# Message passing over a sorted edge list: when GpSimd waits for its scatters in the sort

## The chip, the cores and the metric

One core of one Trainium2 chip runs the whole program. The metric is the device time of one execution in microseconds. The core's engines run side by side: TensorE (PE in the profile, PEld for its weight loads), VectorE (DVE), ScalarE (ACT), GpSimd (POOL) and SyncE (SP, which here only issues DMAs). They meet through semaphores.

## The reference

The input is a graph of 12500 nodes with 128 features and 200000 edges; each edge has a source, a destination, 16 attributes and a type. `src` and `dst` are the edges' ends. The edges arrive sorted by destination.

```python
edge_index = jnp.stack([src, dst])
x = _layernorm(x + _L0(x, edge_index, edge_type_9, ...))   # messages summed per destination, then a GRU cell
x = _layernorm(x + _L1(x, edge_index, edge_attr_16, ...))  # three GIN layers
# _L0: messages = segment_sum(h[src] @ W_msg.T + b_msg + edge_embed[type], dst)
# _L1, per layer: agg = segment_sum(concat(x[dst], edge_attr @ enc_w + enc_b), src), self loops added,
#      then two matrix products with a batch norm and a relu between them
```

Everything that touches edges is a gather of node rows and a sum over the edges of a node. The kernel turns a large part of it into dense products with counts: how many edges lead from a node of one block to a node of another.

## The kernel before, in words

The 200000 edges lie in 1563 tiles of 128 edges, one edge per partition. The program has three stages: the **sort** (which also builds the counts), the first layer with its GRU cell, and three GIN layers. All engines go through the stages in the same order, each with its own program.

**The sort.** The tiles are taken in 25 windows (class `Window`), of 56 tiles in window 0, 64 in windows 1 to 23 and 35 in window 24. For each group of four tiles VectorE makes one-hot rows of the source block (`rank_onehot`, L1976), TensorE counts them up over the partitions (`ranks_tensor`, L2703 to L2709), VectorE copies the carry (L2052), multiplies (L2053, which raises the semaphore `prod` once per group) and reduces (L2065) to the rank of each edge within its source block. At the end of a window `window_places` computes each edge's slot in a table in DRAM and writes it as an integer (L1968), which raises `placed`. Windows 0 and 1 are cut into three and two pieces that are placed one by one.

**The scatters.** GpSimd takes the pieces in order. For each tile it issues one indirect DMA (L3017) that scatters 128 records of 20 words of four bytes, 80 bytes each, from the buffer `RECA` to their slots in the table `RAd` (rec_q in the profile). There are 1563 of them. Before a piece GpSimd waits for `placed` and for the records (`rec_made`, written by ScalarE, three buffers that go round by window). Inside a window the tiles go in fours ("quads"), and two more waits stand there. One paces the scatters of a window beside the ranking of the window after it: at the first tile of a quad GpSimd waits until VectorE has finished a certain group of that window (`ranked_beside`, on `prod`). The other one holds GpSimd to its landings: all scatters of a quad raise one of two semaphores of the buffer, even quads the first and odd quads the second, by 16 each when they have landed (`scat[q % 3][quad % 2]`), and at the second tile of every quad but the first GpSimd waits for all four scatters of the quad before.

**Who waits for the scatters.** ScalarE refills a record buffer only when the scatters of the window three before have landed (`records_scalar`, L2432; it is issued at the seventh group of the window before). SyncE reads the sorted records back for the counts (`cell_records_sync`, L3071 and L3076), two ranges of destinations at a time, when the windows that hold them have landed. The units of this work (375, `cells_vector`, `cells_tensor`, `cells_scalar`, `cells_sync`) start in window 4 and are spread beside the ranking at 18 units a window: VectorE makes one-hot rows (L2028, L2034), TensorE multiplies them into counts (L2733) and multiplies the counts with node features (L2750), ScalarE copies the counts out (L2457, L2461), and SyncE transposes them by DMA (L3115, 360 of them) and stores them (L3124). The next stage starts when all scatters have landed: VectorE, SyncE and GpSimd each wait for that at its head (L2219, L3225, L3024).

**After the sort.** GpSimd gathers node rows for the edges that the counts leave out (L3033 in the first layer, L3051 in the GIN layers); TensorE multiplies counts with node features (L2965). These lines aren't touched by the change.

Of the kernel before, what the change touches and what calls it, by code (L numbers as in the profile page):

```python
# [27 lines left out]
GT = 4  # L28
# [121 lines left out]
def ranked_beside(x, tile):  # L150

    w = x.w if x.b < x.w.n else WIN[x.w.q + 1]
    return x.w.g0 + x.b // GT + (tile - x.first) // GT * w.groups // 16 - 1
# [157 lines left out]
def scattered(q, part):  # L311

    return 16 * sum(1 for i in range(q % 3, q + 1, 3) for k in range(tiles_in(i)) if k // GT % 2 == part)


def scattered_to(q, quad):

    return (scattered(q - 3, quad % 2) if q >= 3 else 0) + 16 * GT * (quad // 2 + 1)
# [61 lines left out]
def summed_beside(r):  # L380

    return max(2 * r - 2, GATHERED[QS0 + r - QR] + 1 if r >= QR else 0)
# [7 lines left out]
def stored(g):  # L390

    return 16 * (g // 2 + 1)


def tiles_of(q, tiles):
    return min(GT, tiles - GT * q)
# [72 lines left out]
def gathered_stored(lay, i):  # L469

    return 16 * max(k // 2 + 1 for k in range(SG * (lay - 1), SG * (lay - 1) + SG - J) if k % 2 == i)
# [1087 lines left out]
def program(nc, x, dst, src, typ, ea, wmsgT, wihT, whhT, emb, bmsg, bih, bhh, encT, w1a, w1b, w2, pv, out):  # L1559
    ctx = ExitStack()  # L1560
    with ctx:
# [5 lines left out]
        def sem(name):  # L1567
            made_sems.append(Sem(ctx.enter_context(nc.semaphore(name))))
            return made_sems[-1]
# [191 lines left out]
        scat = [[sem(f"scattered{i}_{part}") for part in range(2)] for i in range(3)]  # L1761
# [1234 lines left out]
        def quick_gpsimd(g):  # L2996
            g.iota(IOTA[:], [[1, P]], base=0, channel_multiplier=0, allow_small_or_imprecise_dtypes=True).then_inc(*iotas.inc())
            g.iota(DIF[:], [[1, P]], base=0, channel_multiplier=-1, allow_small_or_imprecise_dtypes=True).then_inc(*iotas.inc())
            g.iota(I258[:, :, 0:86], [[86, 3], [1, 86]], base=0, channel_multiplier=0, allow_small_or_imprecise_dtypes=True).then_inc(*iotas.inc())
            g.iota(POSF, [[1, CP]], base=TRASH, channel_multiplier=NTQ, allow_small_or_imprecise_dtypes=True).then_inc(*iotas.inc())  # L3000
            g.iota(N0B, [[P, 100], [0, 16]], base=-P, channel_multiplier=0, allow_small_or_imprecise_dtypes=True).then_inc(*iotas.inc())
            g.iota(IO256[:], [[1, 256]], base=0, channel_multiplier=0, allow_small_or_imprecise_dtypes=True).then_inc(*iotas.inc())
            g.iota(I132[:, :, 0:44], [[44, 3], [1, 44]], base=0, channel_multiplier=0, allow_small_or_imprecise_dtypes=True).then_inc(*iotas.inc())
            g.wait_ge(nulls.sem, 16 * NULLS_FIRST)
            for x in PIECES:
                q, a = x.w.q, WIN[x.w.q - 1].end if x.w.q else 0
                if q == NULLS_FIRST // 2 and x.first == a:
                    g.wait_ge(nulls_rest.sem, 16 * (TRASH // 49 - NULLS_FIRST))
                g.wait_ge(placed.sem, x.n + 1)
                g.wait_ge(rec_made.sem, 3 + 3 * (q + 1))  # L3010
                for c in range(x.first, x.end):
                    quad = (c - a) // GT
                    if q < 24 and (c - x.first) % GT == 0 and ranked_beside(x, c) > x.w.g0 + x.b // GT:
                        g.wait_ge(prod.sem, ranked_beside(x, c))
                    if quad and (c - a) % GT == 1:
                        g.wait_ge(scat[q % 3][(quad - 1) % 2].sem, scattered_to(q, quad - 1))
                    g.indirect_dma_start(  # L3017
                        out=RAd, out_offset=bass.IndirectOffsetOnAxis(ap=POSI[:, c:c + 1], axis=0),
                        in_=RECA[q % 3][:, c - a, :], in_offset=None).then_inc(*scat[q % 3][quad % 2].inc(16))
            for i in range(4):  # L3020
                g.wait_ge(m_out[i].sem, 16 * len(range(i, SG * J, 4)))
            for i in range(3):
                for part in range(2):
                    g.wait_ge(scat[i][part].sem, scattered(24 - (24 - i) % 3, part))  # L3024
            g.wait_ge(weights_dve.sem, 4)
            for i in range(2):
                g.wait_ge(xp_out[i].sem, stored(SG - 1 - i) + 16 * (i == 0))
            for q in range(QS0, NQ0):
                r = q - QS0
                if summed_beside(r) > 0:  # L3030
                    g.wait_ge(q0_sum.sem, summed_beside(r))
                for i in range(tiles_of(q, C)):
                    g.indirect_dma_start(  # L3033
                        out=XG[:, r % QR, i, 0:3 * P], out_offset=None, in_=XPd,
                        in_offset=bass.IndirectOffsetOnAxis(ap=SRCi[:, GT * q + i:GT * q + i + 1], axis=0)).then_inc(*rows_in[r % QR].inc(16))
            g.wait_ge(idx_made.sem, 2 * (NS // IX))
            for i in range(2):
                g.wait_ge(x1_out[i].sem, stored(SG - 1 - i))
                g.wait_ge(pc_out[i].sem, stored(SG - 1 - i))
                g.wait_ge(xt_out[i].sem, stored(SG - 1 - i))  # L3040
            for lay in range(3):
                if lay:
                    for i in range(2):
                        g.wait_ge(hb_out[i].sem, gathered_stored(lay, i))
                for x in GRP[SG * lay:SG * (lay + 1)]:
                    for r in range(x.group0, x.group0 + x.groups):
                        a = K * (4 * x.u + (r - x.group0) // 2) + TO[r % 2]
                        if r >= LR:
                            g.wait_ge(row_sum.sem, r - LR + 1)
                        for i in range(TS[r % 2]):  # L3050
                            g.indirect_dma_start(  # L3051
                                out=GL[:, r % LR, i, 0:3 * P], out_offset=None, in_=HGd[lay],
                                in_offset=bass.IndirectOffsetOnAxis(ap=IDXA[:, a + i:a + i + 1], axis=0)).then_inc(*rows_in[r % LR].inc(16))
            g.wait_ge(row_sum.sem, 3 * QL)
            g.sem_inc(*done.inc())
# [318 lines left out]
        quick_scalar(nc.scalar)  # L3374
        quick_tensor(nc.tensor)
        quick_gpsimd(nc.gpsimd)
        quick_sync(nc.sync)

# [81 lines left out]
```

## Time and profile before

| | |
|---|---|
| time, median of 3 runs | 6228.43 us (6224.02 to 6235.12) |
| span of the profiled execution | 6981.5 us (no other time of this execution is listed) |
| the sort, in the profiled execution | from 0 to 2676.5 us |
| POOL busy, whole span | 4213.9 us (60%), 4243 instructions |
| DVE busy, whole span | 3769.9 us (54%) |
| PE busy, whole span | 5386.3 us (77%) |

A row of the profile names a line, an engine and an operation, the tiles that it writes and reads, and how long the engine was idle ahead of it, with what ended that idle time. "issue" means that the engine waited for nothing that the profile shows. "remote", and on the chain "another core or an unknown queue", means that a semaphore came up at that moment and that no recorded instruction explains when. The profiled execution is 753.1 us longer than the median of the runs.

### The profile page before, as it was taken

The page shows a single profiled execution, that of the slowest core. Times are in us where ns is not written, and L with a number is a line of the kernel's source. Part 1 is how long each engine was busy: PE and PEld are TensorE (multiplying, and loading weights), DVE is VectorE, ACT ScalarE, POOL GpSimd, SP SyncE. Part 2 cuts the span into 40 slices and gives each one's busy share as a digit, 9 for nine tenths or more (in the row PEclk, how much of TensorE's full clock was granted, in tenths as well). Part 3 has the DMA queues.
Part 4 walks back from the last instruction along what each step waited for, and adds up shares of the span by engine and source line. Part 5 has one row for each costly group of instructions (what it writes and reads, how often), then busy time and mean ns, then how long its engine had stood idle before and what let it go on. Part 6 is the DMA issues. An engine that isn't in the chain of part 4 may idle for free.

```text
span 6981.5 us, 88118 instructions
## 1 busy us (share of the span) xinstructions
PE 5386.3 (77%) x26429; PEld 3361.9 (48%) x26429; DVE 3769.9 (54%) x14165; ACT 3302.5 (47%) x4432; POOL 4213.9 (60%) x4243
## 2 busy tenths in 40 slices
PE   4376767676766764666676999999898998898998
PEld 1133333333333322333344666666666666666666
DVE  8576767777766754455566444443333333444443
ACT  1164545555655641122122666665555554554554
POOL 5655555555555556666631666666676666666665
PEclk5588988888988985677776999999999999999999
DMA  7165556556655652333323666667666667666665
GB/s 250 48 144 129 140 121 138 127 134 136 157 127 127 148 138 76 98 101 102 100 78 121 188 190 185 194 196 220 184 186 179 190 191 217 184 184 174 177 185 148
DMA packets 1068177, 1066.40 MB, mean 153 GB/s; under 512 B 494051, under 2 KB 784501, under 8 KB 1067701
## 3 DMA queue, kind: packets, MB, share of 16 engines
q1 hardware_dynamic: 889573, 782.05, 40.1%
q0 software_dynamic: 178128, 278.65, 16.0%
q8 instruction: 220, 3.60, 0.2%
q14 instruction: 256, 2.10, 0.1%
HBM read 747.21 MB, written 216.68 MB: 138 GB/s over the span
## 4 chain that ended last, share of the span: by engine, by line
PE 44%; another core or an unknown queue 6%; DVE 4%; issue 4%; ACT 2%; DMA 1%; SPq 0%; DVEq 0%; ACTq 0%
PE ps L2965 27%; PE ps L2935 4%; PE ps L2848 2%; PE ps L2899 2%; PE ps L2809 2%; PE ps L2810 1%; DVE BIG L2197 1%; PE ps L2909 1%; PE ps L2910 1%; PE ps L2811 1%; ACT MSR L2575 1%; DVE MSR L2258 0%; PE ps L2812 0%; PE ps L2914 0%
## 5 line engine op out<-in xcount | busy, mean ns | idle before, releaser
L3051 POOL DMA_INDIRECT GL<-h_gathered,IDXA x2058 | 2112.6, 1027 | 1227.7 <-issue 568.5
L2965 PE MATMUL ps<-MSR,HP 128*128 128x512 f32 (+1 forms) x9000 | 2375.0, 410 | 174.9 <-ACT MSR L2575 71.2
L3017 POOL DMA_INDIRECT rec_q<-BIG x1563 | 1513.7, 968 | 1156.2 <-issue 473.6
L2575 ACT CAST MSR<-MS 128x1024 fp32r<-128x1024 uint8 (+1 forms) x1500 | 1491.8, 1028 | 1272.9 <-PE ps L2965 820.3
L2965 PEld LDWEIGHTS ps<-MSR,HP 128*128 128x128 f32 x9000 | 1675.6, 195 | 624.9 <-issue 168.5
L2750 PE MATMUL ps<-MTB,XPS 128*128 128x512 bf16 x4410 | 1312.2, 416 | 1.1 <-DMA XPS<-x_parts 0.8
L2258 DVE CAST MSR<-MS 128x1024 fp32r<-128x1024 uint8 (+1 forms) x750 | 522.6, 699 | 1236.7 <-PE ps L2965 738.5
L2457 ACT CAST MT<-ps 128x512 uint16<-128x512 f32 x735 | 427.4, 582 | 959.2 <-remote 633.3
L2461 ACT CAST MTB<-MT 128x1024 bf16<-128x1024 uint8 x735 | 767.9, 1045 | 64.8 <-PE ps L2750 10.3
L3033 POOL DMA_INDIRECT BIG<-x_parts,SRCq x611 | 582.8, 954 | 341.5 <-issue 164.4
L2750 PEld LDWEIGHTS ps<-MTB,XPS 128*128 128x128 bf16 x4410 | 439.7, 103 | 248.7 <-issue 68.1
L2935 PE MATMUL ps<-GL,SL 128*128 128x384 bf16 (+1 forms) x2058 | 456.0, 338 | 8.9 <-issue 7.3
L2709 PE MATMUL ps<-BIG 128*128 128x392 f16 x435 | 165.2, 380 | 354.4 <-DVE BIG L2052 269.1
L2733 PE MATMUL ps<-BIG 128*128 128x256 bf16 x738 | 215.5, 293 | 286.8 <-DVE BIG L2034 83.7
L2034 DVE TENSOR_SCALAR BIG<-I,BIG 128x258 bf16<-128x258 f16 x982 | 335.0, 399 | 188.3 <-remote 162.5
L2197 DVE TENSOR_SCALAR BIG<-IO,DREL 128x256 bf16<-128x256 f16 x1579 | 352.7, 299 | 94.2 <-remote 84.6
L2239 DVE TENSOR_SCALAR SL<-IOTH,RELA 128x128 bf16<-128x128 f16 x2058 | 387.1, 263 | 0.0
L1976 DVE TENSOR_SCALAR BIG<-IOTM,BIG 128x98 f16<-128x98 f16 x1804 | 346.5, 254 | 0.0
L2809 PE MATMUL ps<-WE,BIG 10*128 10x512 f32 x196 | 166.3, 940 | 197.7 <-ACT XMT L2522 158.8
L2052 DVE CAST BIG<-ps 128x98 f16<-128x98 f32 x435 | 109.6, 252 | 306.9 <-remote 288.0
L2733 PEld LDWEIGHTS ps<-BIG 128*128 128x128 bf16 x738 | 77.6, 105 | 395.7 <-issue 179.7
L2935 PEld LDWEIGHTS ps<-GL,SL 128*128 128x128 bf16 x2058 | 154.7, 98 | 229.3 <-issue 166.2
(248 smaller groups left out, 6244.4 us busy)
## 6 DMA issues: line engine op xcount, KB each, us to landing
MS<-counts SPq DMA_DIRECT2D x1080, 256.0 KB
counts<-BIG SPq DMA_DIRECT2D x360, 256.0 KB
XPS<-x_parts SPq DMA_DIRECT2D x192, 384.0 KB
GL<-h_gathered,IDXA POOLq DMA_INDIRECT x2058
rec_q<-BIG POOLq DMA_INDIRECT x1563
rec_q<-BIG SPq DMA_DIRECT2D x44, 490.0 KB, 10.4
HTI<-h_cols SPq DMA_DIRECT2D x72, 256.0 KB
h_dense<-PCL SPq DMA_DIRECT2D x30, 512.0 KB
```

The lines of the kernel that those rows point to most:

```text
L2197: got = v.tensor_scalar(hot[:, i, :], IO256[:, :], DREL[:, GT * q + i:GT * q + i + 1], None, ALU.is_equal)
L2239: got = v.tensor_scalar(SL[:, r % LR, i, :], IOTH[:, :], RELA[:, q + i:q + i + 1], None, ALU.is_equal)
L2258: v.tensor_copy(MSR[:, g % RM, :, 0:w].rearrange("p t (c s) -> p t c s", s=P), MSB[:, i % MR, 0:4 * w].rearrange("p (c h s t) -> p h t c s ...
L2457: s.copy(MT[:, m % 3, 512 * i:512 * (i + 1)].bitcast(U16), PS[PAIR[(p0 + i) % 2]][:, :]).then_inc(*mt_out.inc())
L2461: s.copy(MTB[:, m % 3, 1024 * i:1024 * (i + 1)], MT[:, m % 3, 512 * i:512 * (i + 1)].bitcast(U8)).then_inc(*mtb.inc())
L2575: s.copy(MSR[:, g % RM, :, 0:w].rearrange("p t (c s) -> p t c s", s=P), MSB[:, i % MR, 0:4 * w].rearrange("p (c h s t) -> p h t c s", h=2, ...
L2750: got = t.matmul(PS[6 + x.j % 2][:, :], XPS[:, x.load % 3, i, part, :], MTB[:, m % 3, 512 * i:512 * (i + 1)], start=4 * x.u + i + part == ...
L2935: got = t.matmul(bank[:, 0:w], SL[:, r % LR, i, :], GL[:, r % LR, i, 0:w], start=at + i == 0, stop=at == 1 and i == TS[1] - 1, skip_group_ ...
L2965: got = t.matmul(bank[:, 0:w], HP[:, d, part, :], MSR[:, g % RM, d % 2, 0:w], start=d + part == 0, stop=lay > 0 and d + part == BD, skip_g ...
L3017: g.indirect_dma_start(out=RAd, out_offset=bass.IndirectOffsetOnAxis(ap=POSI[:, c:c + 1], axis=0), in_=RECA[q % 3][:, c - a, :], in_offset ...
L3033: g.indirect_dma_start(out=XG[:, r % QR, i, 0:3 * P], out_offset=None, in_=XPd, in_offset=bass.IndirectOffsetOnAxis(ap=SRCi[:, GT * q + i: ...
L3051: g.indirect_dma_start(out=GL[:, r % LR, i, 0:3 * P], out_offset=None, in_=HGd[lay], in_offset=bass.IndirectOffsetOnAxis(ap=IDXA[:, a + i: ...
```

## The change

GpSimd's wait for its landings moves from the second tile of a quad to the first, and asks for the quad before the last one instead of the last one. It stands from the third quad of a window on. All else is the same: the number of scatters, their order, the semaphores that they raise, and the other waits.

```diff
                     if q < 24 and (c - x.first) % GT == 0 and ranked_beside(x, c) > x.w.g0 + x.b // GT:
                         g.wait_ge(prod.sem, ranked_beside(x, c))
-                    if quad and (c - a) % GT == 1:
-                        g.wait_ge(scat[q % 3][(quad - 1) % 2].sem, scattered_to(q, quad - 1))
+                    if quad >= 2 and (c - a) % GT == 0:
+                        g.wait_ge(scat[q % 3][quad % 2].sem, scattered_to(q, quad - 2))
                     g.indirect_dma_start(
                         out=RAd, out_offset=bass.IndirectOffsetOnAxis(ap=POSI[:, c:c + 1], axis=0),
                         in_=RECA[q % 3][:, c - a, :], in_offset=None).then_inc(*scat[q % 3][quad % 2].inc(16))
```

Before, at most five scatters of a window were on their way at once (a quad and the first of the next); now at most eight. `scattered_to(q, quad)` gives the semaphore's value when that quad of window q has landed.

## Rows read from the trace of the kernel before

**Rows 1.** The page: the span, and the chain of waits by engine.

```profile
span 6981.5 us, 88118 instructions
...
PE 44%; another core or an unknown queue 6%; DVE 4%; issue 4%; ACT 2%; DMA 1%; SPq 0%; DVEq 0%; ACTq 0%
```

**Rows 2.** Line L3017 over the whole span: count, min/median/max ns, what ended idle time.

```profile
L3017 POOL DMA_INDIRECT rec_q<-BIG x1563: 952/958/1733, 22.7 to 2674.4; - x196
...
  DVE BIG L1968: 209.3, 16
```

**Rows 3.** GpSimd's waits up to 302 us: us in total, times, longest us.

```profile
POOL rec_q L3017 <- issue: 53.5, 162, 1.5
POOL rec_q L3017 <- DMA rec_q<-BIG: 36.5, 13, 4.9
```

**Rows 4.** GpSimd's waits from 302 to 2632 us.

```profile
POOL rec_q L3017 <- issue: 410.1, 1155, 4.6
POOL rec_q L3017 <- DMA rec_q<-BIG: 224.2, 126, 4.7
POOL rec_q L3017 <- DVE BIG L2053: 202.1, 55, 12.8
```

**Rows 5.** GpSimd in order of time at the sort's end: start us, us, [idle before].

```profile
2582.26 0.96 POOL L3017 DMA_INDIRECT rec_q<-BIG  x1 [6.82 <-DVE BIG L2053]
...
2591.46 0.96 POOL L3017 DMA_INDIRECT rec_q<-BIG  x1 [3.14 <-DMA rec_q<-BIG]
...
2632.72 0.96 POOL L3017 DMA_INDIRECT rec_q<-BIG  x1 [0.30 <-issue]
...
2674.38 0.96 POOL L3017 DMA_INDIRECT rec_q<-BIG  x1 [0.30 <-issue]
```

**Rows 6.** The chain of waits in order of time there: start us, us, what.

```profile
2674.38 2.09 DMA rec_q<-BIG
```

**Rows 7.** Busy time of each engine, windows 3 to 23 of the ranking.

```profile
core 0: us, PE busy (x) PEld busy (x) DVE busy (x) ACT busy (x) POOL busy (x), PEclk, DMA share, GB/s
302.80:2526.10 2223.30, 1546.48 (x8845) 793.92 (x8845) 1596.81 (x6143) 1198.70 (x1578) 1239.07 (x1285) 0.85 0.58 135
```

**Rows 8.** VectorE's waits in that stretch: us in total, times, longest us.

```profile
DVE BIG L2052 <- remote: 227.7, 64, 10.8
DVE BIG L2034 <- remote: 162.5, 43, 13.1
DVE WE L2034 <- remote: 102.1, 29, 13.3
DVE PC L1994 <- remote: 29.1, 2, 16.9
```

**Rows 9.** VectorE in order of time at the sort's end.

```profile
2593.01 0.56 DVE L2053 TENSOR_TENSOR BIG<-ps,BIG 128x392 f32<-128x392 f32 x1
...
2620.23 0.18 DVE L1968 CAST BIG<-BIG 128x35 int32<-128x35 f32 x1
...
2676.91 0.09 DVE L2221 MEMSET BIG<- 128x1 f32 x2 [36.37 <-DMA rec_q<-BIG]
```

**Rows 10.** VectorE and GpSimd in order of time where window 2's places are ready.

```profile
196.32 0.20 DVE L1968 CAST BIG<-BIG 128x64 int32<-128x64 f32 x1
...
217.38 0.95 POOL L3017 DMA_INDIRECT rec_q<-BIG  x1 [0.30 <-issue]
```

**Rows 11.** ScalarE's waits in the stretch of rows 7.

```profile
ACT BIG L2440 <- DMA BIG<-rec_q: 95.9, 1, 95.9
ACT MT L2457 <- DMA BIG<-MT: 17.1, 9, 2.9
```

**Rows 12.** DMA queues from 1000 to 1250 us: packets, MB, share of 16 engines.

```profile
q0 software_dynamic: 4672, 1.50, 4.0%
...
rec_q<-BIG POOLq DMA_INDIRECT x148
```

**Rows 13.** The same stretch of the ranking: the transposes of the counts.

```profile
L3115 SPq DMA_TRANSPOSE BIG<-MT x360: 1113/1238/3040, 324.4 to 2522.7; - x180
```

## The prediction

> **What bounds the kernel now.** I read the page first for the span and the chain of waits, then the line of the scatters, then the waits by engine for the sort in pieces, then the order of time at the sort's end.
>
> The chain ends at the last scatter: the record of L3017 at 2674.38 us, 2.09 us until it has landed [rows 6], and behind it VectorE, idle for 36.37 us, starts the next stage [rows 9]. So at its end the sort is bound by GpSimd. Before that the profiled execution shows GpSimd waiting for VectorE, not the other way: 202.1 us on its pace [rows 4] and 209.3 us on the places of a window [rows 2]. VectorE in turn is busy for 1596.8 of the 2223.3 us from window 3 to 23 [rows 7] and idle for 521.4 us on "remote" (227.7 + 162.5 + 102.1 + 29.1) [rows 8]. It is full up with work and with waits that no recorded instruction explains.
>
> What is bound in the timed runs is another question, since the profiled execution's span (it lists no other time) is 753 us longer than their median; the sums below are made in the profiled execution and carried over to the median through this difference. Had the two only the unexplained waits between them, then this is how they divide. The chain from 2674 us on holds 6% of the span as "another core or an unknown queue" [rows 1], 419 us (5.5 to 6.5%: 384 to 454). The other 753 - 419 = 334 us (299 to 369) must then be missing from the sort, which takes 2676.5 - 334 = 2342 us (2307 to 2377) in a timed run.
>
> GpSimd's own chain, with no wait for VectorE in it, comes out nearly as long. The last 34 scatters stand 1.262 us apart ((2674.38 - 2632.72) / 33, rows 5): 0.958 of work and 0.30 between. 1563 of them [rows 2] take 1973 us, from 22.7 us on [rows 2]. Waits for landings: up to 302 us 36.5 us in 13 rows [rows 3], less 0.30 each is 33; after that 224.2 in 126 [rows 4], 186. Some of these waits have no releaser and stand under "issue": 53.5 + 410.1 us over 162 + 1155 rows [rows 3, 4], less 0.30 each, 68 more at most. Landings so cost 219 to 287 us, and the whole is 22.7 + 1973 + 219 to 287 + 2.1 = 2217 to 2285 us. Against 2342 (2307 to 2377) GpSimd has 22 to 160 us to spare in 25 windows: about one to six us in a hundred. I take it to be on the path for part of the sort.
>
> **The change, part by part.** It adds and removes no instruction but the wait. Nothing passes another queue: the wait and the scatters stay on GpSimd, in the same order, and what is queued behind the wait is the quad itself, and behind that the next window's, for which ScalarE's refill, SyncE's read-back and the next stage wait.
>
> *The landings.* The old wait costs nothing if the last scatter of a quad lands within two steps, 2.53 us from its start; when it stands, the landing takes those 2.53 us and the wait, less the 0.30 of every step, on top. The mean wait is 224.2 / 126 = 1.8 us, the longest 4.9 [rows 3, 4], so the landings take 4.0 us in the mean and at most 7.1. The new wait asks for that scatter five steps after its start, 6.3 us. The mean landing is there by then; the longest leaves 0.8 us. I put 10 us for what is left in the sort; the ends are 0 and, if landings grow by as much as the scatters run ahead, the old 287. The rows stand near the first: at the quiet end the 34 scatters have no wait at all, 2.09 us to land, and under load 1.8 us more.
>
> The Trainium skill, "DMA: Bandwidth & Descriptors", section "Anatomy of one DMA — SWDGE (gpsimd) path", gives 2.0 us fixed and bytes / 436e3 for such a DMA. For 128 records of 80 bytes that is an estimate of 2.02 us, and by it no landing would reach 2.53 us and the change would remove nothing. The trace agrees for the quiet end (2.09) and disagrees beside the other queues (139 waits that end with a landing); what happens if the rule holds in timed runs is the third rival.
>
> *What is late next.* VectorE's ranking and units. Their floor in those 2223.3 us [rows 7, 8] is that time less the unexplained waits, 1702; the timed runs' own, all 334 us taken from there, is 1889. GpSimd's in it falls from 1285 x 1.262 = 1622 plus 186 to 246, 1808 to 1868, to about 1630. So the gain there lies between 0 (VectorE, held by real waits for TensorE, already makes the 1889) and 187 (GpSimd holds it there, and VectorE would do it in its floor). No row tells which, as the waits that would replace the unexplained ones are hidden in them; I take the middle, 93 us, because the two chains at 1889 and 1868 lie side by side.
>
> *The sort's end.* In the profiled execution GpSimd's tenth quad of window 23 starts at 2582.26 behind VectorE [rows 5]. Without landings the next two follow at 5.05 us each; the twelfth needs the group that VectorE ends at 2593.57 [rows 9], so it starts at 2593.9, and its 20 scatters end at 2619.1. Window 24 is placed at 2620.41 [rows 9]; its 35 scatters start at 2620.7, the last at 2663.6 instead of 2674.38. That is 11 us, and VectorE's 36.37 us of idle time cover it.
>
> *The start.* Window 2's places are ready at 196.5 us; GpSimd comes to them at 217.38 [rows 10], late by the landings of windows 0 and 1. 21 us at most are to be had there, as before 196.5 it would wait for VectorE. ScalarE's 95.9 us wait for the first records read back [rows 11] shows that these scatters then hold the units; in the profiled execution VectorE's own pace takes the place of most of it.
>
> Both are within the 93 us where GpSimd binds, and stand alone where it doesn't.
>
> **The forecast.** 6228 - 93 = 6135 us. In its own case (GpSimd on the path) 6050 to 6200.
>
> **The rivals.**
> 1. *VectorE paces the timed sort as it does the profiled one.* For it: 411 us of GpSimd's waits are for VectorE. Against: the 2217 to 2285 us above leave it little. Gain: the end's 11 us, and 0 to 21 from the start: 6197 to 6217, say 6210.
> 2. *Slower: the scatters that run ahead hold up the transposes.* Each scatter costs each of the 16 engines 4.0% x 250 us / 148 = 0.068 us of packets [rows 12]. With up to four more on their way, a transpose that meets them all is 0.27 us late, and ScalarE's copies wait for it; 360 transposes [rows 13] make 97 us, 6325. Against: there are no more scatters than before, and ScalarE waits for transposes by name for 17.1 us only [rows 11]. It decides when it eats the 11 us of the end, so from one transpose in nine on; at one in three, 33 - 11: 6250.
> 3. *The change doesn't do what it says:* in timed runs the landings come within 2.53 us, as at the quiet end, and there is no wait to remove: 6228, 6223 to 6233. For it: landings are slower in the profile if its own records load the queues. Against: the DMA share in the sort is 0.58 [rows 7], and that load is the kernel's.
>
> **How the numbers follow.** Forecast 0.48, rival 1 0.33, rival 3 0.10, rival 2 0.09. Faster by over 0.2% (12.5 us, about what a measurement here can tell from no change): all of the forecast and three quarters of rival 1, 0.73. Within 0.2%: the rest of rival 1 and rival 3, 0.18. Slower: 0.09. The range runs from 6055 (a gain near the 187 leaves out 0.06) to 6232 (leaves out rival 2 and a little of rival 3).
>
> **What would show it.** The line of the scatters should lose nearly all idle time that ends with a landing of rec_q, 260 us to some 10, and in its place idle time on VectorE's L2053 and L1968 should grow. In the profile, whose unexplained waits hold VectorE, the sort should then end only 11 to 30 us sooner; the timed median should fall by more than the span does. VectorE's idle time ahead of the next stage should fall from 36 to about 25 us. It is wrong if landings still hold GpSimd (scatters in flight slow each other), if the "remote" waits stand in timed runs too (then 6210), or if SyncE's transposes and ScalarE's copies take longer.

## The result and the profile after

| | median us | of runs | lowest to highest |
|---|---|---|---|
| before | 6230.41 | 4 | 6224.02 to 6235.12 |
| after | 5871.65 | 4 | 5867.58 to 5877.86 |

The ratio is 0.9422 [0.9401, 0.9443]: 359 us less. The change is much faster than the forecast of 6135 us, and the time lies below the range that was given (6055 to 6232).

The profile that the rows come from can't be laid beside the one after the change. The kernel before was profiled once more, unchanged (the first of the experiments below), and this second profile has a span of 6232.5 us where that execution took 6235.53 us. All "remote" waits of [rows 8] are gone in it. So the first profile was of a disturbed execution; what disturbed it is open. From here on "before" is the second profile, unless rows are named.

The page of each kernel: the span, and the chain by engine. First before (second profile), then after; they answer to [rows 1].

```profile
span 6232.5 us, 88118 instructions
...
PE 39%; POOL 13%; issue 4%; DMA 2%; DVE 1%; ACT 1%; SPq 1%; DVEq 0%; ACTq 0%
```

```profile
span 5868.0 us, 88444 instructions
...
PE 44%; POOL 10%; issue 4%; DMA 3%; DVE 2%; ACT 1%; SPq 1%; DVEq 0%; ACTq 0%
```

No unknown queue is left on the chain of either.

The line of the scatters over the whole span, as in [rows 2]. Before (second profile):

```profile
L3017 POOL DMA_INDIRECT rec_q<-BIG x1563: 952/958/1737, 22.7 to 2413.0; - x196
its engine sat idle before it (us, times) until:
  issue: 448.6, 1317
  DMA rec_q<-BIG: 426.5, 221
  DVE BIG L1968: 17.3, 1
  DVE BIG L2053: 7.3, 24
```

After:

```profile
L3017 POOL DMA_INDIRECT rec_q<-BIG x1563: 952/958/1733, 22.7 to 2040.1; - x196
its engine sat idle before it (us, times) until:
  issue: 443.4, 1447
  DMA rec_q<-BIG: 37.1, 84
  DVE BIG L1968: 29.4, 5
  DVE BIG L2053: 11.8, 27
```

The number and the duration of the scatters are unchanged. Idle time that ends with a landing falls from 426.5 us in 221 pieces to 37.1 in 84. In neither profile does GpSimd wait for VectorE to speak of, where [rows 2] and [rows 4] showed 209 and 202 us of it; 17.3 us stand before the very first scatter. With 0.30 us of each piece counted as the ordinary step, the landings cost 426.5 - 221 x 0.30 = 360 us before, and 53 more stand under "issue" (448.6 - 1317 x 0.30): 413. So GpSimd's chain is 22.7 + 1973 + 413 + 2.1 = 2411 us, and the next stage starts at 2415.5. That all of GpSimd's time adds up to the sort is no wonder; what the sum tells is that nothing of it is left for VectorE. After, the landings are 12 us (37.1 - 84 x 0.30), 9 more stand under "issue", and waits for VectorE behind the first scatter are 15 (12.1 + 11.8 - 31 x 0.30): 22.7 + 1973 + 36 + 2.1 = 2034 us, and the next stage starts at 2042.7.

The stretch of windows 3 to 23 of the ranking, engine by engine, which answers to [rows 7]. Before (second profile), then after:

```profile
core 0: us, PE busy (x) PEld busy (x) DVE busy (x) ACT busy (x) POOL busy (x), PEclk, DMA share, GB/s
219.90:2236.90 2017.00, 1436.40 (x8845) 767.26 (x8845) 1583.72 (x6143) 1197.89 (x1581) 1263.89 (x1313) 0.87 0.64 149
```

```profile
222.10:1889.10 1667.00, 1411.00 (x8845) 758.14 (x8845) 1580.40 (x6145) 1196.09 (x1578) 1251.13 (x1296) 0.97 0.78 180
```

350 of the 364.5 us between the two spans are in this one row. It starts at nearly the same time in both (219.9 and 222.1), so nothing is gained ahead of it; another 25 us are gained from its end to the next stage (178.6 and 153.6 us). Every engine is busy for nearly as long in both; only the time between is shorter. VectorE is now busy for 1580 of 1667 us, 95%. TensorE's mean granted clock is 0.97 of the 2.4 GHz level where it was 0.87; its busy time falls by 25 us with that, so the clock can't be what gave back the 350. The runs of the kernel before bear that out: over the span they show a mean clock of about 0.91 or about 0.885, and take the same time with either (6237.47 us at 0.910, 6231.46 at 0.887).

How GpSimd's lateness reached the others is in the waits. ScalarE up to the sort's end (us in total, times, longest), before and then after; [rows 11] had the same view of a shorter stretch:

```profile
ACT BIG L2432 <- DMA rec_q<-BIG: 395.0, 18, 45.6
...
ACT BIG L2440 <- DMA BIG<-rec_q: 85.7, 1, 85.7
...
ACT MT L2457 <- DMA BIG<-MT: 25.8, 3, 21.7
```

```profile
ACT BIG L2440 <- DMA BIG<-rec_q: 84.7, 1, 84.7
...
ACT BIG L2432 <- DMA rec_q<-BIG: 38.9, 5, 12.3
...
ACT MT L2457 <- DMA BIG<-MT: 10.5, 4, 3.6
```

TensorE in the stretch of windows 3 to 23, before and after:

```profile
PE ps L2733 <- ACT MT L2457: 335.3, 22, 25.6
```

```profile
PE ps L2733 <- ACT MT L2457: 20.7, 9, 5.5
```

VectorE behind its wait for the first records read back, before (396 to 2295 us) and after (359.4 to 1946.4 us):

```profile
DVE BIG L1982 <- ACT BIG L2440: 93.3, 9, 23.7
DVE BIG L2034 <- PE ps L2733: 87.0, 13, 19.6
DVE BIG L1986 <- ACT BIG L2444: 72.6, 5, 22.5
DVE WE L2034 <- PE ps L2733: 51.7, 6, 20.4
```

```profile
DVE BIG L1982 <- ACT BIG L2440: 13.3, 6, 5.2
DVE BIG L1986 <- ACT BIG L2444: 5.3, 2, 3.5
```

One such turn of before in order of time, on ScalarE, TensorE and VectorE:

```profile
1098.08 1.11 ACT L2432 COPY BIG<-BIG 128x1024 f32<-128x1024 f32 x1 [21.20 <-DMA rec_q<-BIG]
```

```profile
1100.12 0.37 PE L2733 MATMUL ps<-BIG 128*128 128x256 bf16 x1 [15.97 <-ACT MT L2457]
```

```profile
1102.06 0.72 DVE L2034 TENSOR_SCALAR BIG<-I,BIG 128x258 bf16<-128x258 f16 x2 [13.18 <-PE ps L2733]
```

It reads so: GpSimd is late with a window, so ScalarE stands for 21.20 us at the refill of that record buffer (L2432); its copies of the counts (L2457) are queued behind that, so TensorE's count products find no free PSUM for 15.97 us (L2733), and VectorE's one-hot rows no free buffer for 13.18 (L2034). ScalarE is held at L2432 in 18 waits, some 22 us each. So VectorE's ranking runs at GpSimd's pace by way of ScalarE, and no row of VectorE's up to the sort's end names the scatters.

The sort's end on VectorE, which answers to [rows 9], and the chain there, as in [rows 6]. After, in order of time:

```profile
1946.22 0.18 DVE L1968 CAST BIG<-BIG 128x35 int32<-128x35 f32 x1
...
2042.68 0.09 DVE L2221 MEMSET BIG<- 128x1 f32 x2 [77.58 <-DMA rec_q<-BIG]
```

```profile
2040.15 2.13 DMA rec_q<-BIG
```

And before (second profile):

```profile
2295.04 0.38 DVE L1968 CAST BIG<-BIG 128x35 int32<-128x35 f32 x1
...
2415.49 0.09 DVE L2221 MEMSET BIG<- 128x1 f32 x2 [102.45 <-DMA rec_q<-BIG]
```

GpSimd still ends the sort in both; VectorE is idle ahead of the next stage for 102 us and then 78, not for 36. From the next stage on the two profiles are alike: 6232.5 - 2415.5 = 3817 us and 5868.0 - 2042.7 = 3825.

The DMA queues from 1000 to 1250 us (packets, MB, share of 16 engines), as in [rows 12]. Before (second profile), then after:

```profile
q1 hardware_dynamic: 68493, 36.62, 62.3%
q0 software_dynamic: 5088, 1.64, 4.6%
```

```profile
q1 hardware_dynamic: 81953, 44.41, 75.6%
q0 software_dynamic: 6252, 2.01, 5.1%
```

GpSimd's queue moves 23% more in the same 250 us and the other queue is at 75.6%, and still nearly all landings are there after five steps.

### The profile page after: what moved, and what is told of

Its sections match the earlier page's. It is cut to its first block, busy times and chain, and to the rows that moved or that the text cites. A ratio compares the mean times of both kernels' runs of the same rounds, so it can differ in the third digit from the quotient of the medians.

```text
span 5868.0 us, 88444 instructions
## 1 busy us (share of the span) xinstructions
PE 5116.0 (87%) x26429; PEld 3281.9 (56%) x26429; DVE 3763.8 (64%) x14165; ACT 3325.4 (57%) x4432; POOL 4223.4 (72%) x4243
## 4 chain that ended last, share of the span: by engine, by line
PE 44%; POOL 10%; issue 4%; DMA 3%; DVE 2%; ACT 1%; SPq 1%; DVEq 0%; ACTq 0%
PE ps L2965 27%; POOL GL L3051 7%; PE ps L2935 5%; POOL BIG L3033 3%; PE ps L2848 2%; PE ps L2809 2%; PE ps L2899 2%; PE ps L2810 2%; DVE BIG L2197 1%; PE ps L2909 1%; PE ps L2910 1%; DMA MS<-counts 1%; PE ps L2811 1%; DMA h_dense<-PCL 1%; PE ps L2914 0%
## 5 line engine op out<-in xcount | busy, mean ns | idle before, releaser
L2965 PE MATMUL ps<-MSR,HP 128*128 128x512 f32 (+1 forms) x9000 | 2292.0, 402 | 56.0 <-ACT MSR L2575 36.6
L2575 ACT CAST MSR<-MS 128x1024 fp32r<-128x1024 uint8 (+1 forms) x1500 | 1509.3, 1029 | 959.0 <-PE ps L2965 867.5
L2965 PEld LDWEIGHTS ps<-MSR,HP 128*128 128x128 f32 x9000 | 1644.5, 190 | 449.4 <-ACT MSR L2575 57.9
L3017 POOL DMA_INDIRECT rec_q<-BIG x1563 | 1514.0, 969 | 521.6 <-issue 443.4
L2750 PE MATMUL ps<-MTB,XPS 128*128 128x512 bf16 x4410 | 1195.2, 387 | 1.0 <-DMA XPS<-x_parts 0.8
L2457 ACT CAST MT<-ps 128x512 uint16<-128x512 f32 x735 | 427.4, 582 | 343.6 <-PE ps L2733 328.9
L2750 PEld LDWEIGHTS ps<-MTB,XPS 128*128 128x128 bf16 x4410 | 414.7, 98 | 216.3 <-issue 20.0
L2034 DVE TENSOR_SCALAR BIG<-I,BIG 128x258 bf16<-128x258 f16 x982 | 330.7, 398 | 1.4 <-PE ps L2733 1.4
L2848 PE MATMUL ps<-BIG 128*128 128x393 bf16 x1203 | 243.9, 358 | 71.8 <-DMA BIG<-x_parts,SRCq 71.8
L2725 PE MATMUL ps<-BIG 128*128 128x51 bf16 x1104 | 210.4, 191 | 59.0 <-DVE BIG L2028 55.0
L2525 ACT ACTIVATE MTB<-ps 128x256 f32<-128x256 f32 x98 | 37.5, 383 | 389.2 <-PE ps L2812 389.2
L2053 DVE TENSOR_TENSOR BIG<-ps,BIG 128x392 f32<-128x392 f32 x451 | 250.8, 556 | 3.6 <-PE ps L2709 3.6
```

The lines of the kernel that those rows point to most:

```text
L2457: s.copy(MT[:, m % 3, 512 * i:512 * (i + 1)].bitcast(U16), PS[PAIR[(p0 + i) % 2]][:, :]).then_inc(*mt_out.inc())
L2575: s.copy(MSR[:, g % RM, :, 0:w].rearrange("p t (c s) -> p t c s", s=P), MSB[:, i % MR, 0:4 * w].rearrange("p (c h s t) -> p h t c s", h=2, ...
L2750: got = t.matmul(PS[6 + x.j % 2][:, :], XPS[:, x.load % 3, i, part, :], MTB[:, m % 3, 512 * i:512 * (i + 1)], start=4 * x.u + i + part == ...
L2965: got = t.matmul(bank[:, 0:w], HP[:, d, part, :], MSR[:, g % RM, d % 2, 0:w], start=d + part == 0, stop=lay > 0 and d + part == BD, skip_g ...
L3017: g.indirect_dma_start(out=RAd, out_offset=bass.IndirectOffsetOnAxis(ap=POSI[:, c:c + 1], axis=0), in_=RECA[q % 3][:, c - a, :], in_offset ...
```

## The experiments

Two theories stood after the result. By the first, GpSimd is on the path through the whole sort of an undisturbed execution, and the time is its landings. By the second, VectorE's pace is the bound, and the landings matter at a few places (the start and the end). Later ones ask what the changed kernel is bound by. Each run is also read at one place: the time of L2221, where the next stage starts. The diffs are against the changed kernel.

**The kernel before, once more, for its profile.** No edit.

> The kernel before, unchanged, for a second profile: the first one's span (6981.5 us) was 753 us over the timed runs and full of waits with no releaser. Theory G (in timed runs GpSimd's scatters bound the sort, landing waits included): the span comes to about 6230 us, GpSimd loses about 360 us to landings in the sort (5871.65 against 6230.41), waits for VectorE under 60 us in windows 3 to 24, and VectorE stands idle over 60 us at the sort's end. Rival V (VectorE paced the sort as in the first profile, and the gain comes from elsewhere, such as transposes that run freer): GpSimd waits for VectorE some 300 us or more, and landings cost it no more than the 219 to 287 us of the first profile.

6235.53 us, with 6241.02 the median of the same kernel's runs beside it. The rows are above: landings 426.5 us, VectorE almost never waited for. That bears out the first theory. It also shows that sizes read from the first profile were not those of a timed run.

**One step to land.** All of the last quad must have landed at a quad's first tile.

```diff
-                    if quad >= 2 and (c - a) % GT == 0:
-                        g.wait_ge(scat[q % 3][quad % 2].sem, scattered_to(q, quad - 2))
+                    if quad and (c - a) % GT == 0:
+                        g.wait_ge(scat[q % 3][(quad - 1) % 2].sem, scattered_to(q, quad - 1))
```

> Only the place changes, the wrong way: the first tile of a quad waits for the last quad (one step of 1.26 us for the landing instead of two). G: each of some 366 waits grows by 0.49 us (a quiet landing of 1.75 us less 1.26) to 1.26 us, so 180 to 460 us on top of before: 6410 to 6690 us. V: GpSimd has 400 us to spare beside VectorE, so most of it is hidden: 6230 to 6300 us.

6750.95 us (6743.52 to 6761.85), ratio 1.0823 [1.0802, 1.0843]: 510 us slower than before, somewhat more than the range had. GpSimd's waits (us, times, longest):

```profile
POOL rec_q L3017 <- DMA rec_q<-BIG: 896.9, 329, 6.6
```

Less 0.30 each these are 798 us against 360, and the next stage starts at 2917.4 instead of 2415.5: 438 of the 502 us are waits that end with a landing by name. The way by ScalarE holds VectorE too (ScalarE's waits at L2432 go from 395.0 us to 797.3), and so GpSimd's waits for VectorE's L2053 come to 101 us, 91 more than the steps; 26 us fewer stand under "issue". Were VectorE the bound, an added wait on GpSimd would have cost little; it costs in full. The range began too low: no run shows a quiet landing of 1.75 us. The shortest in the traces takes 2.09, so each of the 366 waits grows by 0.83 us at least, and the range should have begun near 6545.

**Three and four steps to land.** The old wait, at the third and at the fourth tile of a quad.

```diff
-                    if quad >= 2 and (c - a) % GT == 0:
-                        g.wait_ge(scat[q % 3][quad % 2].sem, scattered_to(q, quad - 2))
+                    if quad and (c - a) % GT == 2:
+                        g.wait_ge(scat[q % 3][(quad - 1) % 2].sem, scattered_to(q, quad - 1))
```

The other one has `== 3` in that place.

> The wait for the last quad at the third tile: three steps, 3.79 us. G: between the second tile's 6241 and the fourth's 5891 us, and nearer the fourth, as most landings in the sort take 2.5 to 4 us: 5940 to 6040 us.

> The wait stays on the last quad, but stands at the fourth tile: four steps, 5.05 us, for the landing, and at most seven scatters on their way. G: landings over 5 us are rare (longest waits of 4.9 us stand for 7.1 us), so nearly the whole gain comes without asking for an older quad: 5865 to 5920 us. V: no change from before in what VectorE does; 6150 to 6230 us.

5994.81 us (5989.99 to 6003.84), ratio 0.9606 [0.9585, 0.9626], and 5891.07 (5887.64 to 5895.22), ratio 0.9439 [0.9423, 0.9454]. Both lie in their ranges. The third tile first, then the fourth:

```profile
POOL rec_q L3017 <- DMA rec_q<-BIG: 195.3, 147, 4.4
```

```profile
POOL rec_q L3017 <- DMA rec_q<-BIG: 62.3, 65, 3.1
```

One step later already takes away 249 us (from 6244.06 for the kernel before, measured beside it), two steps 350 (from 6241.02). It is the steps that a landing gets which count, not which semaphore or quad is asked for.

**No wait for landings inside a window.** The two lines go. The buffers' other waits stay.

```diff
-                    if quad >= 2 and (c - a) % GT == 0:
-                        g.wait_ge(scat[q % 3][quad % 2].sem, scattered_to(q, quad - 2))
```

> No wait for landings inside a window at all (the records' buffers and the stage's head still wait for all). G: the changed kernel's GpSimd has only some 12 us of landing waits left in 84 places, so 5860 to 5875 us against its 5871.65. A rival within G, that more scatters on their way slow each other or the transposes: over 5885 us.

5866.05 us (5859.54 to 5871.78), ratio 0.9403 [0.9388, 0.9419]. Without the two lines the scatters stand on L3015, and no row of theirs names a landing any more:

```profile
POOL rec_q L3015 <- issue: 467.5, 1533, 0.3
POOL rec_q L3015 <- DVE BIG L1968: 40.5, 10, 17.3
POOL rec_q L3015 <- DVE BIG L2053: 7.7, 20, 1.9
```

The gaps under "issue" are now 0.3 us each, the ordinary step, and what is left beside them are waits for VectorE. The time lies in the range and 6 us under the changed kernel's, so the change has taken all but a few us of what landings cost, and the rival by which more scatters on their way slow each other or the transposes (over 5885 us) falls.

**The changed kernel and the one without the wait, once more.** No edit to the first; the second as above.

> The changed kernel again, beside the next one on the same chip: 5865 to 5885 us, and a ratio to before of 0.940 to 0.944.

> No landing wait inside a window, again. If the changed kernel's last 12 us of landing waits count in full (G): 5 to 15 us under the run before this one. If VectorE, which is right behind, takes their place (N): within 5 us of it.

5877.81 us (5870.49 to 5885.58), ratio 0.9413 [0.9396, 0.9430], and 5869.75 (5868.18 to 5877.61), ratio 0.9400 [0.9383, 0.9416]. The intervals of the two ratios overlap, and in the two profiles the next stage starts at 2041.5 and 2042.7 us, with no gain at all. So whether leaving the wait out is better still is not settled, and theories G and N can't be told apart here.

**The new wait in the first half of the sort, the old one in the second.**

```diff
-                    if quad >= 2 and (c - a) % GT == 0:
+                    if q < 12 and quad >= 2 and (c - a) % GT == 0:
                         g.wait_ge(scat[q % 3][quad % 2].sem, scattered_to(q, quad - 2))
+                    if q >= 12 and quad and (c - a) % GT == 1:
+                        g.wait_ge(scat[q % 3][(quad - 1) % 2].sem, scattered_to(q, quad - 1))
```

> The new wait in windows 0 to 11, the old one in windows 12 to 24. G: GpSimd bounds the sort throughout, so the landing waits of windows 12 to 24 in the second profile of before (199 us) come back and no more: 5872 + 199 = 6071, within 6045 to 6095 us. A rival, that VectorE, ahead by then, or the records' buffers absorb part of them: below 6020 us.

6062.68 us (6058.51 to 6067.20), ratio 0.9712 [0.9692, 0.9732]. That is about half of the gain, and in the range: 181 us from 6244.06 for the kernel before, measured beside it, where the changed kernel gives 359 to 371:

```profile
POOL rec_q L3019 <- DMA rec_q<-BIG: 225.3, 154, 5.0
```

So the landings bind in both halves alike. That the gain is not one of the start or the end of the sort stands in the row of windows 3 to 23 above, with its 350 us.

**Fewer scatters in the changed kernel: what is late next?** In windows 3 to 23 every eighth scatter is left out, 168 in all, so these edges' records are missing from the table. What the waits count to is lowered to match (not shown), and the kernel's own test of the number of edges is answered as if they were there.

```diff
+def left_out(q, k):
+    return 3 <= q <= 23 and k % 8 == 7
...
                 for c in range(x.first, x.end):
...
+                    if left_out(q, c - a):
+                        continue
```

> The changed kernel without every eighth scatter of windows 3 to 23 (168 of 1563; their records are missing from the table, and the later check of the edge count is answered as if they were there). GpSimd issues 168 x 1.262 = 212 us less. Theory N (VectorE is right behind GpSimd: it was busy for 1580 of 1667 us in windows 4 to 23 of the changed kernel): the sort then ends with VectorE's last places (1946 us in the changed kernel, at most 27 us sooner by ScalarE's waits for landings) and the 35 scatters of window 24 behind them, 44 + 2 us: 1966 to 1993 instead of 2042 us, so 5796 to 5822 us. Rival F (VectorE only follows GpSimd's pace and has room below it, as it had when its windows went from 98 to 81 us): nearly all of the 212 us, 5660 to 5700 us.

5818.90 us (5817.11 to 5821.21), ratio 0.9320 [0.9301, 0.9338]. 168 x 1.262 = 212 us of GpSimd's work are gone, and the time falls by 53 (against 5871.65). GpSimd's waits up to the sort's end (lines stand 7 to 9 lower here; L1975 is L1968):

```profile
POOL rec_q L3026 <- DVE BIG L1975: 163.2, 22, 17.3
POOL rec_q L3026 <- DMA rec_q<-BIG: 56.8, 68, 4.0
```

Now GpSimd waits for the places of each window. VectorE's places of window 24 come at 1928.65 us instead of 1946.22: 18 us is all that it still had to give, and the rest of the 53 is the shorter tail behind it, 41.31 us of idle time instead of 77.58:

```profile
1928.65 0.18 DVE L1975 CAST BIG<-BIG 128x35 int32<-128x35 f32 x1
...
1988.05 0.09 DVE L2228 MEMSET BIG<- 128x1 f32 x2 [41.31 <-DMA rec_q<-BIG]
```

So the forecast in which GpSimd alone binds (5660 to 5700) falls, and the one in which VectorE is right behind (5796 to 5822) holds. VectorE waits for others for only 11 us in all here from 300 to 1930 us: its own work sets the pace, and in the changed kernel GpSimd held it back by no more than those 18 us up to the last window.

All runs in order of the room that a landing has (the start is that of the profiled execution):

| steps from a quad's last scatter to its wait | next stage starts at us | median us | median less that start |
|---|---|---|---|
| 1 | 2917.4 | 6750.95 | 3834 |
| 2 (before, one run) | 2415.5 | 6235.53 | 3820 |
| 5 in windows 0 to 11, then 2 | 2233.0 | 6062.68 | 3830 |
| 3 | 2165.8 | 5994.81 | 3829 |
| 4 | 2064.7 | 5891.07 | 3826 |
| 5 (the change) | 2042.7 | 5871.65 | 3829 |
| 5 (the change, once more) | 2041.5 | 5877.81 | 3836 |
| no wait | 2036.2 | 5866.05 | 3830 |
| no wait, once more | 2042.7 | 5869.75 | 3827 |
| 4 or 5, with 168 scatters left out | 1988.1 | 5818.90 | 3831 |

The last column is the same for all within 16 us. All that these edits do to the time, they do to the sort.

## Why the prediction was wrong in size

*What the wait does was right; how much of the sort hangs on it was not.* The wait moved by three steps takes away the landings; 10 us were to be left over, and 12 are by name, 21 with those under "issue". Landings hardly grow when the scatters run ahead. The traces hold the times at which the semaphores rise: by these the last scatter of a quad lands 3.2 us after its start in the mean before, 3.5 after and 3.5 with no wait; the longest take some 8.5 us, more than the 7.1 of the prediction, and are few. GpSimd is on the path, but all through the sort and not for part of it. The last landing takes 2.13 us (2.09 in the prediction). The rival in which the transposes are slowed is not borne out: ScalarE's waits for them are 10.5 us after, 25.8 before. The rival in which there is nothing to remove fails at 221 waits. VectorE pacing the sort (the first rival) fails at the 7 us that GpSimd waits for L2053. The forecast had counted the Trainium skill's rule ("DMA: Bandwidth & Descriptors", section "Anatomy of one DMA — SWDGE (gpsimd) path", an estimate of 2.02 us) towards the third rival, in which there is nothing to remove: it agrees with the 2.13 us at the quiet end and not with 221 waits, of up to 6.6 us, that stand behind the two steps beside the other queues.

*The first step that failed is the division of the 753 us*, 419 behind the sort and 334 within. The second profile has 3817 us behind the sort where the first has 4305, so 488 and 261 of the 749 us between the two profiles. A sort without the disturbance is 2415 us long, not 2342 (2307 to 2377). The row that was used is the chain's share of unexplained waits [rows 1], and the disturbance also lengthened the time that is not on that share.

*The second is the landings, 219 to 287 us.* They are 413. The count was right for the profiled execution [rows 3, 4] and was carried over as if it held for any. But while VectorE's unexplained waits held GpSimd back, landings came in their shade: 139 waits that end with a landing there, 221 in the undisturbed one, and a fuller DMA (0.64 against 0.58). GpSimd's chain so comes to 2411 us and fills the sort of 2415; the "22 to 160 us to spare" were 4. That the stalls cast this shade is read from the two profiles; no run set them going by itself. This is the term that weighs most: with the division alone put right, the prediction's 2217 to 2285 us in a sort of 2415 would have left GpSimd 130 to 198 us to spare, and VectorE would have looked the bound.

*The third is the 93 us, the middle between 0 and 187*, taken since no row told which engine held the stretch. GpSimd held all of it. VectorE's stretch was to be 1889 us with a floor of 1702; it was 2017 and came down to 1667, 350 us. The floor is off by 35 only. The 1808 to 1868 us of GpSimd beside it were 14 too many: the 186 to 246 us of landings in them belong to the longer stretch of [rows 4], and in windows 3 to 23 the first profile has 173 to 232 (208.5 us in 117 waits, and 389.4 us in 1101 under "issue", less 0.30 each). Had the whole sort been taken as GpSimd's, the sum would have been 413 us of landings less 12 and 9 left over and 15 of waits for VectorE, 377, against the 373 by which the next stage starts earlier. With the prediction's own landings it could not have come to more than 287 less 10, 277.

*The start and the tail.* The 0 to 21 us at the start were 0, as windows 3 to 23 start no sooner, and ScalarE's wait for the first records read back stays (85.7 and 84.7 us). VectorE's idle time of 36 us was to fall to about 25. It is 102 before and 78 after, since an undisturbed VectorE is further ahead at the end. Among the signs, L2053 and L1968 were to grow as reasons of GpSimd's waits; together they go from 24.6 to 41.2 us only, and to 180 with 168 scatters fewer. And the span did not fall by less than the median: 364.5 us from the second profile, 359 in the medians.

## What to carry to other kernels

A profile whose span is far above the timed median, with waits that no recorded instruction ends, can name a mechanism but not its size: what it counts of a wait is a lower bound wherever another engine's stalls lie over it, so the range has to reach to the case without cover. A wait for a landing costs only what the landing takes beyond the steps that run meanwhile; the first step added to it is worth most. And the engine that is late may show up on others only through a third: VectorE's rows named ScalarE and TensorE, and it was the buffer that GpSimd hadn't emptied.

## What the runs showed of the hardware

- A scatter of 128 records of 80 bytes takes GpSimd 0.958 us in the median and 0.30 between, however many are on their way: the step is the same with two or five steps to land and with no wait at all.
- Its landing takes 2.13 us at the sort's end, where the DMA share is 0.06. In the mean of the whole sort the last scatter of a quad takes 3.2 us before and 3.5 after. Beside a DMA share of 0.64 GpSimd still waits for it after two steps (2.53 us) in 221 cases, for up to 6.6 us; with a share of 0.78 in the changed kernel, after five steps (6.3 us), in 84, for up to 3.1 us.
- What the landings cost the kernel falls steeply with each step that they get, from one step on: by 510 us (6750.95 to 6241.02), 249 (6244.06 to 5994.81), 104 (5994.81 to 5891.07) and 13 to 19 (5891.07 to 5877.81 or 5871.65).
- TensorE's mean granted clock over the span is higher in the kernels in which it waits less, at the same 26429 matmuls: 0.883 in most runs with one step to land, 0.91 before, 0.926 with three steps, 0.934 after. In some executions of a kernel it is 0.02 to 0.03 lower (0.855, 0.885 and 0.911 for one step, before and after), with no difference in the time that stands out.
